# One attention turn in a new sequence on all five engines, with both row sends of a tile behind TensorE's query transposes

## The chip, the cores and the metric

The kernel runs on one core of one Trainium2 chip. The metric is the device time of one execution in microseconds (us); the span of a profiled execution is a little shorter than its time.

## The reference, cut to what matters

`x` is (64, 64, 256) and `ctx` is (64, 64, 256), both fp32. B = L = 64, D = 256, 16 heads of 16, 8 experts with inner size 176, two experts per token.

```python
q = rms_norm(linear(layernorm(x), q_w, q_b), norm_q_w)      # over all 256
k = rms_norm(linear(ctx, k_img_w, k_img_b), norm_k_img_w)
v = linear(ctx, v_img_w, v_img_b)
x = x + linear(attention(q, k, v), o_w, o_b)                # 16 heads, softmax(q k / 4) v
h = layernorm(x)
topw, sel = top_k(softmax(h @ gate_w.T), 2)                 # topw divided by its sum
out = x + sum over the two experts of topw * w2 @ (silu(g) * u)   # g, u = halves of w1 @ h
```

All context tokens fall under the image weights, since L is below 257; the text branch sees no tokens.

## The kernel before

**Stages.** 4096 tokens are 32 tiles of 128 tokens (two batches of 64). A first stage runs attention, the second LayerNorm and the routing, tile by tile, and writes each normalised row twice, once for each of its two experts, into `sorted_rows` in HBM, at a place that depends on the routing. A plan of 72 expert slots follows, then the expert stage reads `sorted_rows` slot by slot and writes `expert_out`; at the end both results of a token are added to `x1`. The change touches the first stage alone.

**Turns.** `turns_sp(eng, turn)` calls `turn(i // 4, i % 4)` for i = 0 to 37 (`LAST`) on every engine; all is unrolled. In turn i an engine works on several tiles at once: `tile(lag)` is tile i - lag, and is left out where it is below 0 or above 31. The order in which `turn` names its steps is the order of the engine's instruction stream; each engine works through it strictly in that order, and semaphores join the engines. So one pass through the five lists is one turn, and takes each of six or more tiles a step further.

**TensorE (PE) in turn i:** `tr_x(i)` (transposes of the normalised input, L1134), `tr_k(i-1)` (L1143), `score_max(i-2)` (rough scores for the row maximum, L1165), `weigh(i-3)` (probabilities times v, 32 small matmuls, L1177), `tr_q(i-1)` (the query transposes, L1150), `project_kv(i)`, `project_q(i)` (helper lines L1117 to L1125), `tr_max(i-2)` (L1206), in odd turns `count_rows`, `tr_att(i-3)` (L1212), `score(i-2)` (L1227 to L1231), `project_out(i-3)` (L1117 to L1125).

**ScalarE (ACT):** `xt_hi(i)`, `k_hi(i-1)` (L554), `ln1_norm(i+1)`, `ctx_hi(i+1)` (L569), `q_hi(i-1)` (four copies, L564), `neg_max_rows(i-2)` (L586), `k_square(i)` (L593), `q_square(i)` (L599), `att_hi(i-3)`, `v_copy(i)`, `weights_hi(i)` (L574), `k_scale(i)` (waits for POOL's `r_qk`, L628), `row_copy(i-4)` (L581), `softmax_exp(i-2)` (L621), in odd turns `gap_exp`.

**VectorE (DVE):** `xt_lo(i)` (L829), `k_lo(i-1)` (L835), `find_max(i-2)` (L846), LayerNorm statistics of tile i+2, the negated maximum, `invert_sums` and `normalise(i-3)`, `q_lo(i-1)` (L841), `ln2_norm(i-4)` (L905), `att_lo(i-3)`, in odd turns `route`, `gate_of_x(i)`, `q_scale(i)` (waits for `r_qk`, L883), `residual(i-3)` (L892 to L896 and the aggregate L899), in even turns `choose` (the two experts of two tiles, L914 to L927).

**GpSimd (POOL):** `ctx_lo(i+1)` (L401), `ln1(i+2)` (L413, L415, L422), `qk_rms(i)` (`ms_eps` L413 and `r_qk` L415; waits for both squares of tile i), in even turns `weights` of two tiles (L442 to L446), `send(i-6)`: a copy of the row numbers (L451) and two indirect DMAs of 128 rows (L457), `ln2(i-3)` (L413, L415), `weights_lo(i)` (L407).

**SyncE (SP)** issues `load_ctx(i+2)`, `load_weights(i+1)` and `spread_v(i)` (four DMAs, L335, which wait for `weighed` of tile i-2).

What binds these lists across engines: `weigh(i-3)` and `score_max(i-2)` wait for `softmax_exp(i-3)`, whose bank of scores `score_max` overwrites; `softmax_exp` stands behind `k_scale` in ACT's list; `tr_k` waits for `k_scale` of its tile; `tr_q` waits for `k_lo` of its tile. After the last turn the routing counts go through 15 small steps on DVE, and SP reads the first 12 rows of the plan into registers (L361) before it waits for all sends and loads the first slot.

Of the kernel before, what the change touches and what calls it, by code (L numbers as in the profile page):

```python
# [7 lines left out]
ALU = mybir.AluOpType  # L8
# [10 lines left out]
B, L, D = 64, 64, 256  # L19
# [66 lines left out]
def build_in(nc, stack, x, ctx_t, w_proj, w_out, w_exp, w_gate, bias, norm_q, norm_k, out,  # L86
# [216 lines left out]
    def _(sp):  # L303
# [39 lines left out]
        def turn(j, s):  # L343
            if Tile(j, s + 2).live:
                load_ctx(Tile(j, s + 2))
# [9 lines left out]

        turns_sp(sp, turn)
# [30 lines left out]
    def _(pool):  # L387
# [37 lines left out]
        def qk_rms(t):  # L425
# [3 lines left out]
            inv_sqrt(t, r_qk[:, t.par, :], ms_eps[:, t.par, :], sumsq[:, t.par, :], 1.0 / D, 1e-6,  # L429
                     S["k_squared"], S["qk_veps"], S["qk_rstd"])  # L430

        def ln2(t):
            need_alone(pool, pool_passed, S["row_ready"], t.n - 1)
            inv_sqrt(t, rstd2[:, t.slot, :], veps2[:, t.par, :], mean_var2[:, t.par, 1:2], 1.0, 1e-5,
                     S["ln2_mean"], S["ln2_veps"], S["ln2_rstd"])
# [12 lines left out]
        def send(t):  # L448
# [3 lines left out]
                             ).then_inc(S["ids_set"], 1)  # L452
            need_alone(pool, pool_passed, S["ids_set"], t.n + 1)
            need_alone(pool, pool_passed, R["place_set"], t.pair + 1)
            need_alone(pool, pool_passed, R["weight_set3"], t.pair + 1)
            for k in range(2):
                pool.indirect_dma_start(  # L457
                    sorted_rows, bass.IndirectOffsetOnAxis(ap=place_i[:, t.slot // 2, k, t.par:t.par + 1], axis=0),
                    row[:, k, t.slot, :], None, bounds_check=ROWS - 1, oob_is_err=False
                ).then_inc(row_sent[t.slot], 16)  # L460
# [985 lines left out]
```

## Time and profile before

| | |
|---|---|
| median of 3 runs | 549.66 us (548.14 to 552.85) |
| the profiled execution: its time, its span | 549.9 us, 548.1 us |
| granted TensorE clock, mean over the span | 0.938 of full |
| PE, PEld, DVE busy | 438.2, 389.1, 413.4 us |
| ACT, POOL busy | 315.5, 303.5 us |

How to read it: the times of the three runs and that of the profiled execution are of the whole program; busy time is the time in which an engine had an instruction running, and PEld (weight loads) overlaps PE. The first stage runs from the start to about 337 us, the expert stage from about 352 us.

### The profile page before, as it was taken

To read this page: it belongs to the slowest core of one execution; us is meant where nothing else is said; L and a number is where in the kernel's file an instruction comes from. 1 tells how busy PE (TensorE), PEld (TensorE's weight loads), DVE (VectorE), ACT (ScalarE), POOL (GpSimd) and SP (SyncE) were. 2 spreads that over 40 slices of the span, in tenths; PEclk is the share of its full clock that TensorE was granted. 3 is DMA by queue.
4 is the path that set the end of the run, shared out by engine and by line. 5 is a ranking of instruction groups with operands and counts; after the bars stand their busy time and mean duration, and the time that the engine had idled before them with its cause. 6 is when DMAs were issued, how large, how long until landed. Compare 5 with 4: busy or idle time off the path is not lost.

```text
span 548.1 us, 14646 instructions
## 1 busy us (share of the span) xinstructions
PE 438.2 (80%) x4120; PEld 389.1 (71%) x4120; DVE 413.4 (75%) x1359; ACT 315.5 (58%) x934; POOL 303.5 (55%) x531
## 2 busy tenths in 40 slices
PE   2879889898989998898989772299999999999100
PEld 1668778777877877787778661199999999899100
DVE  7458888988988898889888867066767676676384
ACT  5357777767776867686777531155656666565000
POOL 6634467777777677767776646224444444444200
PEclk9989999999999999999999986599999999999655
DMA  7231432222322222222222113524444444331499
GB/s 232 53 111 40 133 129 83 73 65 80 88 67 72 74 82 73 77 78 77 79 72 74 50 50 94 149 81 129 124 123 126 119 121 126 111 115 66 168 401 351
DMA packets 49560, 60.51 MB, mean 110 GB/s; under 512 B 7616, under 2 KB 43083, under 8 KB 49483
## 3 DMA queue, kind: packets, MB, share of 16 engines
q1 hardware_dynamic: 38026, 38.00, 23.7%
q0 software_dynamic: 6528, 16.86, 8.8%
q10 hardware_dynamic: 4928, 4.72, 2.6%
q8 instruction: 37, 0.61, 0.5%
q14 instruction: 41, 0.33, 0.2%
HBM read 32.86 MB, written 23.27 MB: 102 GB/s over the span
## 4 chain that ended last, share of the span: by engine, by line
PE 62%; DVE 12%; issue 7%; ACT 5%; POOL 5%; DMA 4%; SPq 2%; another core or an unknown queue 0%; POOLq 0%; ACTq 0%; DVEq 0%
PE bank L1117 11%; PE bank L1118 11%; PE bank L1119 11%; PE bank L1328 4%; DMA we_l<-expert_out 3%; PE bank L1177 3%; PE bank L1125 3%; PE bank L1150 3%; PE bank L1227 2%; DVE late L835 2%; PE bank L1231 2%; PE bank L1228 2%; PE bank L1229 2%; PE bank L1165 2%; PE bank L1357 1%
## 5 line engine op out<-in xcount | busy, mean ns | idle before, releaser
L527 POOL DMA_INDIRECT expert_out<-probs,late x72 | 70.0, 972 | 94.4 <-ACT probs L720 60.1
L457 POOL DMA_INDIRECT sorted_rows<-row,place_i x64 | 66.0, 1031 | 36.2 <-POOL row L451 24.5
L564 ACT CAST qp_h<-bank 32x256 f16<-32x256 f32 x128 | 46.4, 363 | 40.8 <-PE bank L1150 38.5
L841 DVE TENSOR_TENSOR qp_l<-bank,qp_h 32x256 f16<-32x256 f32 x128 | 53.7, 419 | 9.8 <-ACT qp_h L564 6.6
L1117 PE MATMUL bank<-we_h,xt_h 128*128 x144 | 53.4, 371 | 0.1
L1075 DVE SCALAR_TENSOR_TENSOR probs<-xn,late,bank 128x128 f32<-128x128 f32 x72 | 25.0, 347 | 36.2 <-issue 16.9
L708 ACT ACTIVATE xn<-bank 128x176 f32<-128x176 f32 x72 | 22.9, 318 | 42.7 <-PE bank L1119 35.2
L1118 PE MATMUL bank<-we_l,xt_h 128*128 x144 | 47.1, 327 | 0.0
L1119 PE MATMUL bank<-we_h,xt_l 128*128 x144 | 46.9, 326 | 0.0
L1067 DVE TENSOR_TENSOR xt_l<-bank,xt_h 128x256 fp32r<-128x256 f32 x72 | 30.5, 424 | 21.3 <-ACT xt_h L702 17.5
L1328 PE MATMUL bank<-ident,late 128*128 128x128 f32 x144 | 30.4, 294 | 18.4 <-DMA late<-sorted_rows 16.2
L415 POOL TENSOR_TENSOR rstd<-veps,half_neg 128x1 f32<-128x1 f32 x64 | 36.8, 575 | 5.5 <-POOL veps L413 0.2
L846 DVE TENSOR_REDUCE bank<-bank 128x16 f32<-128x1024 f32 x32 | 39.1, 1221 | 0.0
L702 ACT CAST xt_h<-bank 128x256 fp32r<-128x256 f32 x72 | 27.1, 376 | 18.9 <-PE bank L1328 18.4
L1227 PE MATMUL bank<-qp_h,late 128*128 128x256 f16 x128 | 35.7, 279 | 2.5 <-ACT neg_max_t L586 0.4
L720 ACT COPY probs<-bank 128x256 f32<-128x256 f32 x72 | 26.8, 373 | 17.6 <-PE bank L1358 10.5
L1177 PE MATMUL bank<-v_bd,probs 128*64 128x34 f32 x1024 | 36.0, 225 | 0.2 <-ACT probs L621 0.2
L1231 PE MATMUL bank<-neg_max_t,head_of 128*128 128x128 bf16 x256 | 35.6, 221 | 0.0
L1228 PE MATMUL bank<-qp_l,late 128*128 128x256 f16 x128 | 35.3, 276 | 0.0
L1229 PE MATMUL bank<-qp_h,late 128*128 128x256 f16 x128 | 35.3, 276 | 0.0
L1177 PEld LDWEIGHTS bank<-v_bd,probs 128*64 128x64 f32 x1024 | 32.4, 138 | 3.6 <-ACT probs L621 0.4
L621 ACT ACTIVATE probs<-bank 128x1024 f32<-128x1024 f32 x32 | 32.8, 1025 | 2.3 <-PE bank L1231 2.3
(199 smaller groups left out, 1594.7 us busy)
## 6 DMA issues: line engine op xcount, KB each, us to landing
late<-sorted_rows SPq DMA_DIRECT2D x72, 129.0 KB
we_f<-w_exp SPq DMA_DIRECT2D x32, 152.0 KB
v_bd<-v_sb SPq DMA_DIRECT2D x128, 34.0 KB, 1.9
ctx_in<-ctx_t SPq DMA_DIRECT2D x32, 128.0 KB
we_h<-expert_out SPq DMA_DIRECT2D x8, 512.0 KB, 6.8
we_l<-expert_out SPq DMA_DIRECT2D x8, 512.0 KB, 15.7
x<-x SPq DMA_DIRECT2D x3, 1024.0 KB, 5.8
out<-we_h ACTq DMA_DIRECT2D x8, 256.0 KB, 13.0
```

The costliest lines, as they stand in the source:

```text
L457: pool.indirect_dma_start(sorted_rows, bass.IndirectOffsetOnAxis(ap=place_i[:, t.slot // 2, k, t.par:t.par + 1], axis=0), row[:, k, t.slot ...
L527: pool.indirect_dma_start(expert_out, bass.IndirectOffsetOnAxis(ap=hs[:, r, D:D + 1].bitcast(U32), axis=0), y_sb[:, r % YRING, :], None, b ...
L564: act.copy(q_part(qp_h, t, g), q_bank(g)).then_inc(S["q_h_ready"], 1)
L841: dve.tensor_tensor(q_part(qp_l, t, g), q_bank(g), q_part(qp_h, t, g), ALU.subtract).then_inc(S["q_l_ready"], 1)
L1117: pe.matmul(dst, a_h, b_h, start=start, stop=False)
L1118: pe.matmul(dst, a_h, b_l, start=False, stop=False)
L1119: return pe.matmul(dst, a_l, b_h, start=False, stop=stop)
L1177: ins = pe.matmul(av_bank[b * L:(b + 1) * L, g * 2 * VW:(g + 1) * 2 * VW], probs[:, t.par, at:at + L], v_bd[:, t.par, b, :, g * VW:(g + 1) ...
L1227: pe.matmul(dst, k_h, q_h, start=True, stop=False)
L1228: pe.matmul(dst, k_h, q_l, start=False, stop=False)
L1231: ins = pe.matmul(dst[:, gh * P:(gh + 1) * P], head_of[:, (b * KC + c) * NQ // 2 + gh, :], neg_max_t[:, t.par, :], start=False, stop=gh == ...
L1328: ins = pe.transpose(bank[:, p, c * P:(c + 1) * P], hs[:, r, c * P:(c + 1) * P], ident[:, :])
```

## The change

The five lists are reordered. Nothing that is computed changes.

- **POOL:** `send` is split. `set_ids(i-5)` (the copy of the row numbers) ends the turn; the two indirect DMAs of tile i-6 now open the next turns' lists, behind a new wait of POOL for `q_transposed`, min(i, 32), which `tr_q(i-1)` raises in the same turn. Behind them stand `ln2_veps(i-4)`, `ctx_lo(i+2)`, `ln1_root(i+2)`, `ln2_root(i-4)`, and only then `qk_rms(i)`. `weights` moves to odd turns and to the end, `ln2` is a tile later.
- **ACT:** `weights_hi` moves up behind `q_hi`, `ctx_hi` is a tile further ahead and stands behind `neg_max_rows`, `ln1_norm` stands behind `att_hi`, `gap_exp` ahead of `k_scale`, `softmax_exp` ahead of `row_copy`, and `k_hi(i)`, `xt_hi(i+1)` end the turn.
- **DVE:** `k_lo` stands ahead of `xt_lo`; the aggregate of the second LayerNorm leaves `residual` and becomes `ln2_mean(i-4)`; the first LayerNorm's statistics are a tile further ahead; `ln2_norm` stands behind `route`, `q_scale` ahead of `gate_of_x`.
- **PE:** `weigh` stands ahead of `score_max`, `tr_max` between `project_kv` and `project_q`, and `tr_k(i)`, `tr_x(i+1)` end turn i (`tr_k` first).
- **SP:** `load_ctx` is a tile further ahead. A few steps of the first tiles move ahead of turn 0.

```diff
@@ SP
         def turn(j, s):
-            if Tile(j, s + 2).live:
-                load_ctx(Tile(j, s + 2))
+            if Tile(j, s + 3).live:
+                load_ctx(Tile(j, s + 3))
...
+        load_ctx(Tile(0, 2))
@@ POOL
-        def send(t):
+        def set_ids(t):
             need_alone(pool, pool_passed, S["row2_ready"], t.n + 1)
             pool.tensor_copy(row[:, :, t.slot, D:D + 1].bitcast(I32), result_row[:, :, bass.ds(t.n, 1)]
                              ).then_inc(S["ids_set"], 1)
+
+        def send(t, k):
             need_alone(pool, pool_passed, S["ids_set"], t.n + 1)
             need_alone(pool, pool_passed, R["place_set"], t.pair + 1)
             need_alone(pool, pool_passed, R["weight_set3"], t.pair + 1)
-            for k in range(2):
-                pool.indirect_dma_start(...)
+            pool.indirect_dma_start(...)
...
         def turn(j, s):
-            if Tile(j, s + 1).live:
-                ctx_lo(Tile(j, s + 1))
+            i = j * SKEW + s
+            if Tile(j, s - 6).live:
+                need(pool, S["q_transposed"], min(i, NT))
+                send(Tile(j, s - 6), 0)
+                send(Tile(j, s - 6), 1)
+            if Tile(j, s - 4).live:
+                ln2_veps(Tile(j, s - 4))
             if Tile(j, s + 2).live:
-                ln1(Tile(j, s + 2))
+                ctx_lo(Tile(j, s + 2))
+            if Tile(j, s + 2).live:
+                ln1_root(Tile(j, s + 2))
+            if Tile(j, s - 4).live:
+                ln2_root(Tile(j, s - 4))
             if Tile(j, s).live:
                 qk_rms(Tile(j, s))
-            if s % 2 == 0 and Tile(j, s - 6).live:
-                weights(Tile(j, s - 6), Tile(j, s - 5), (s - 6) // 2 % 2)
-            if Tile(j, s - 6).live:
-                send(Tile(j, s - 6))
-            if Tile(j, s - 3).live:
-                ln2(Tile(j, s - 3))
             if Tile(j, s).live:
                 weights_lo(Tile(j, s))
+            if Tile(j, s + 2).live:
+                ln1_shift(Tile(j, s + 2))
+            if s % 2 == 1 and Tile(j, s - 5).live:
+                weights(Tile(j, s - 5), Tile(j, s - 4), (s - 5) // 2 % 2)
+            if Tile(j, s - 5).live:
+                set_ids(Tile(j, s - 5))
@@ ACT
-            xt_hi(tile(0)); k_hi(tile(1)); ln1_norm(tile(-1)); ctx_hi(tile(-1))
             q_hi(tile(1))
+            weights_hi(tile(0))
             neg_max_rows(tile(2))
+            ctx_hi(tile(-2))
             k_square(tile(0)); q_square(tile(0)); att_hi(tile(3))
+            ln1_norm(tile(-1))
             v_copy(tile(0))
-            weights_hi(tile(0))
+            if s % 2 == 1: gap_exp(tile(5), tile(4), ...)
             k_scale(tile(0))
+            softmax_exp(tile(2))
             row_copy(tile(4))
-            softmax_exp(tile(2))
-            if s % 2 == 1: gap_exp(tile(5), tile(4), ...)
+            k_hi(tile(0)); xt_hi(tile(-1))
@@ DVE
-            xt_lo(tile(0)); k_lo(tile(1)); find_max(tile(2)); ln1_stats(tile(-2))
-            neg_max_hi(tile(2)); invert_sums(tile(3)); neg_max_lo(tile(2)); normalise(tile(3)); ln1_mean(tile(-2))
-            q_lo(tile(1)); ln2_norm(tile(4)); att_lo(tile(3)); route(...)
-            gate_of_x(tile(0)); q_scale(tile(0)); residual(tile(3)); choose(...)
+            k_lo(tile(1)); xt_lo(tile(0)); find_max(tile(2)); ln2_mean(tile(4))
+            neg_max_hi(tile(2)); neg_max_lo(tile(2)); invert_sums(tile(3)); ln1_mean(tile(-2)); ln1_stats(tile(-3)); normalise(tile(3))
+            q_lo(tile(1)); att_lo(tile(3)); route(...); ln2_norm(tile(4))
+            q_scale(tile(0)); gate_of_x(tile(0)); residual(tile(3)); choose(...)
@@ PE
-            tr_x(tile(0)); tr_k(tile(1)); score_max(tile(2)); weigh(tile(3)); tr_q(tile(1))
-            project_kv(tile(0)); project_q(tile(0)); tr_max(tile(2))
+            weigh(tile(3)); score_max(tile(2)); tr_q(tile(1))
+            project_kv(tile(0)); tr_max(tile(2)); project_q(tile(0))
             count_rows(...); tr_att(tile(3)); score(tile(2)); project_out(tile(3))
+            tr_k(tile(0)); tr_x(tile(-1))
```

The parts for ACT, DVE and PE are written here one call behind the other, without their `if tile(n).live`.

## Rows read from the trace of the kernel before

**Rows 1.** The page: busy time of each engine.

```profile
PE 438.2 (80%) x4120; PEld 389.1 (71%) x4120; DVE 413.4 (75%) x1359; ACT 315.5 (58%) x934; POOL 303.5 (55%) x531
```

**Rows 2.** Stretches A:B (us): length, busy per engine, granted clock, DMA share.

```profile
191.81:210.57 18.76, 17.11 (x195) 14.68 (x191) 16.65 (x60) 13.50 (x40) 13.99 (x28) 1.00 0.27 75
310.00:320.00 10.00, 7.52 (x97) 6.12 (x96) 7.58 (x23) 5.90 (x14) 6.97 (x12) 1.00 0.17 55
```

**Rows 3.** Timeline of PE: query transposes of tiles 5, 21, 22, 23, 31.

```profile
71.09 0.41 PE L1150 MATMUL bank<-ident,late 128*128 128x128 f32 x2 [0.17 <-DVE late L835]
...
220.33 0.41 PE L1150 MATMUL bank<-ident,late 128*128 128x128 f32 x2 [0.17 <-issue]
...
230.01 0.41 PE L1150 MATMUL bank<-ident,late 128*128 128x128 f32 x2 [0.91 <-DVE late L835]
...
238.94 0.41 PE L1150 MATMUL bank<-ident,late 128*128 128x128 f32 x2 [0.17 <-issue]
...
313.45 0.44 PE L1150 MATMUL bank<-ident,late 128*128 128x128 f32 x2
```

**Rows 4.** Timeline of PE: what stands ahead of the transposes at 230.01.

```profile
227.44 0.61 PE L1165 MATMUL bank<-late,qp_h 128*128 128x128 f16 x8 [0.29 <-ACT probs L621]
227.98 1.13 PE L1177 MATMUL bank<-v_bd,probs 128*64 128x34 f32 x32
```

**Rows 5.** Timeline of ACT: k_scale, row copy, exponential, k_hi, two q_hi.

```profile
225.60 0.47 ACT L628 ACTIVATE late<-bank,r_qk 128x256 f32<-128x256 f32 x1 [0.38 <-POOL r_qk L415]
225.97 0.40 ACT L581 COPY row<-row 128x256 f32<-128x256 f32 x1
226.27 1.02 ACT L621 ACTIVATE probs<-bank 128x1024 f32<-128x1024 f32 x1
...
227.44 0.61 ACT L554 CAST late<-bank 128x512 f16<-128x512 f32 x1
...
230.79 1.52 ACT L564 CAST qp_h<-bank 32x256 f16<-32x256 f32 x4 [1.96 <-PE bank L1150]
...
239.38 1.52 ACT L564 CAST qp_h<-bank 32x256 f16<-32x256 f32 x4 [0.52 <-PE bank L1150]
```

**Rows 6.** Timeline of POOL in one turn, and one second send.

```profile
217.59 1.09 POOL L457 DMA_INDIRECT sorted_rows<-row,place_i  x1 [0.82 <-POOL row L451]
218.98 0.97 POOL L457 DMA_INDIRECT sorted_rows<-row,place_i  x1 [0.30 <-DVE mean_var L899]
220.02 0.19 POOL L413 TENSOR_SCALAR veps<-mean_var 128x1 f32<-128x1 f32 x1
220.29 0.57 POOL L415 TENSOR_TENSOR rstd<-veps,half_neg 128x1 f32<-128x1 f32 x1
...
221.65 0.74 POOL L401 TENSOR_TENSOR ct_l<-ctx_in,ct_h 128x256 fp32r<-128x256 f32 x1
...
224.58 0.19 POOL L413 TENSOR_SCALAR ms_eps<-sumsq 128x2 f32<-128x2 f32 x1 [0.80 <-ACT square L599]
224.86 0.71 POOL L415 TENSOR_TENSOR r_qk<-ms_eps,half_neg 128x2 f32<-128x2 f32 x1
...
229.13 0.97 POOL L457 DMA_INDIRECT sorted_rows<-row,place_i  x1 [0.30 <-issue]
```

**Rows 7.** Timeline in the expert stage: the copy on ACT that POOL's indirect DMA awaits.

```profile
402.50 0.37 ACT L720 COPY probs<-bank 128x256 f32<-128x256 f32 x1 [0.23 <-PE bank L1358]
...
403.64 0.97 POOL L527 DMA_INDIRECT expert_out<-probs,late  x1 [1.06 <-issue]
```

**Rows 8.** Timeline of DVE at the end of that turn: residual, and k_lo.

```profile
226.53 0.42 DVE L892 TENSOR_TENSOR x<-bank,x 128x256 f32<-128x256 f32 x1 [0.45 <-PE bank L1125]
...
229.19 0.68 DVE L835 TENSOR_TENSOR late<-bank,late 128x512 f16<-128x512 f32 x1
```

**Rows 9.** The chain that ended last: SP's register loads, then the first slot's load.

```profile
349.58 0.15 SPq L361
...
350.13 2.15 DMA late<-sorted_rows
```

More of the change, by code:

```diff
@@ L495, in _ @@
                                  base=0, pattern=[[1, NE], [-1, NE]], channel_multiplier=0))
-        ln1(Tile(0, 0))
-        ln1(Tile(0, 1))
+        for n in range(2):
+            ln1_root(Tile(0, n))
+            ln1_shift(Tile(0, n))
         ctx_lo(Tile(0, 0))
@@ L521, in _ @@
                         ).then_inc(q_cleared, 1)
+        ctx_lo(Tile(0, 1))
         turns_sp(pool, turn)
@@ L645, in tile @@
                 return t
-            if tile(0).live:
-                xt_hi(tile(0))
-            if tile(1).live:
-                k_hi(tile(1))
-            if tile(-1).live:
-                ln1_norm(tile(-1))
-            if tile(-1).live:
-                ctx_hi(tile(-1))
             if tile(1).live:
@@ L693, in _ @@
         ln1_norm(t)
+        xt_hi(t)
+        ctx_hi(Tile(0, 1))
         split_hi(1)
@@ L989, in turn @@
                 route(tile(5), tile(4), (s - 5) // 2 % 2)
-            if isinstance(j, int) and j == s == 0:
+            if tile(4).live:
+                ln2_norm(tile(4))
+            if n == 0:
                 fold_gate()
             if tile(0).live:
+                q_scale(tile(0))
+            if tile(0).live:
                 gate_of_x(tile(0))
-                q_scale(tile(0))
             if tile(3).live:
@@ L1284, in seen @@
                 return min(value, NT) if static else value
-            if tile(0).live:
-                tr_x(tile(0))
-            if tile(1).live:
-                tr_k(tile(1))
+            if tile(3).live:
+                weigh(tile(3))
             if tile(2).live:
@@ L1293, in turn @@
                 score_max(t)
-            if tile(3).live:
-                weigh(tile(3))
             if tile(1).live:
                 tr_q(tile(1))
-            if tile(0).live:
+            if static and i == 0:
                 t = tile(0)
-                t.first = static and i == 0
-                for project_next in (project_q, project_kv) if t.first else (project_kv, project_q):
-                    project_next(t)
-            if static and i == 0:
+                t.first = True
+                project_q(t)
+                project_kv(t)
                 gate_fold()
+            elif tile(0).live:
+                t = tile(0)
+                t.first = False
+                project_kv(t)
             if tile(2).live:
@@ L1308, in turn @@
                 tr_max(t)
+            if tile(0).live and not (static and i == 0):
+                t = tile(0)
+                t.first = False
+                project_q(t)
             if s % 2 == 1 and tile(5).live:
@@ L1318, in turn @@
                 project_out(t)
+            if tile(0).live:
+                tr_k(tile(0))
+            if tile(-1).live:
+                tr_x(tile(-1))
         gate_mean()
+        tr_x(Tile(0, 0))
         turns_sp(pe, turn)
```

74 lines of the change are left out of this document (42 added, 32 removed).

## The prediction

> **What bounds the kernel now.** I read the page first: PE is busy 80% and DVE 75% of the span, POOL 55% [rows 1]. None is full, so the windows come next. Over two whole turns of 18.76 us PE is busy 17.11 and DVE 16.65 us, ACT and POOL some 14 us, at granted clock 1.00 [rows 2]: a turn costs 9.4 us, of which PE works 8.6 and DVE 8.3. From the query transposes of tile 5 to those of tile 31 there are 26 turns and 313.45 - 71.09 = 242.4 us [rows 3], 9.32 us a turn. The turns alternate: 230.01 - 220.33 = 9.68 us where DVE's `choose` stands ahead of `k_lo`, and 238.94 - 230.01 = 8.93 us where it doesn't [rows 3]. PE loses two things in a turn: 0.29 us waiting for the exponential ahead of `score_max` [rows 4], and 0.17 or 0.91 us waiting for `k_lo` ahead of `tr_q` [rows 3]. The reader is to see how small this is: if both went, 0.46 and 1.20 us, a turn would cost 8.5 us on PE, and no order can give back more than (9.32 - 8.5) x 26 = 21 us.
>
> POOL is not on this loop now. Its `qk_rms` sits idle 0.80 us until the query square is there [rows 6], then `k_scale` starts 0.03 us after `r_qk` [rows 5, 6]. The sends stand behind `qk_rms`, where nothing of the same turn waits for what follows them.
>
> **The change, what it removes.** `k_lo` ahead of `xt_lo` and the aggregate taken out of `residual` bring `k_lo` forward by some 0.4 us. `softmax_exp` ahead of `row_copy` brings the exponential forward by 0.30 us (226.27 - 225.97) [rows 5]. Both aim at PE's two waits; alone they would give most of 0.8 us in a long turn and 0.3 in a short one. `tr_max` ahead of `project_q`, `weights_hi` and `ctx_hi` in ACT's idle time cost and give nothing by themselves: ACT has 1.96 or 0.52 us of idle ahead of `q_hi` [rows 5] and the new steps fill it. `weigh` ahead of `score_max` moves work among neighbours; `find_max` gets its scores a `weigh` later, but it has the negated maximum due only after `project_kv`. `load_ctx` has more than a turn of slack.
>
> **What it adds: a loop through POOL.** This is the term that decides. In turn i POOL now waits for `tr_q(i-1)` of the same turn, sends twice, does four steps, and only then computes `r_qk(i)`; ACT's `k_scale(i)` and, behind it in the list, `softmax_exp(i-2)` wait for that; `weigh(i-2)` and `score_max` on PE wait for the exponential; behind them stands `tr_q(i)`, for which POOL waits again. All steps are in one order on their engine, so the sum of this loop is a floor for the turn. With 0 at the end of `tr_q(i-1)`:
> - From the wait to the first indirect DMA: 0.77 us, the distance from the end of the copy that POOL awaits to its DMA in the expert stage (403.64 - 402.87) [rows 7]; in this stage 0.82 us stand behind the copy of row numbers [rows 6]. I take 0.80.
> - The two sends: 1.09 + 0.30 + 0.97 = 2.36 us, and 0.07 to the next step (220.02 - 219.95) [rows 6]. At 3.23.
> - `ln2_veps` 0.19, `ctx_lo` 0.74, `ln1_root` 0.27 + 0.57, `ln2_root` 0.57, `qk_rms` 0.28 + 0.71 [rows 6]: 3.33 us, less some 0.06 of overlaps. `r_qk` is there at 6.5 us. Before it was there at 225.57 - 220.74 = 4.83 us [rows 3, 6].
> - `k_scale` starts at 6.53, the exponential one step of 0.37 us (225.97 - 225.60) later, at 6.90, and takes 1.02 [rows 5]: 7.92 us.
> - PE begins `weigh` 0.15 us after it (227.44 - 227.29) [rows 4, 5], at 8.07. `weigh` and `score_max` take 229.11 - 227.44 = 1.67 us together [rows 4] and `tr_q` 0.41, less 0.06 of overlap: 10.09 us.
>
> In even turns `choose` makes it longer. `q_scale` starts with `k_scale` at 6.53, `residual` about 0.6 later at 7.12. From `residual` to `k_lo` it is 2.66 us now (229.19 - 226.53) [rows 8]; without `xt_lo` (0.34 of issue) and without the aggregate (about 0.2) it is 2.1. `k_lo` ends at 7.12 + 2.1 + 0.68 = 9.9, PE starts `tr_q` 0.14 later and ends it at 10.45. In odd turns `k_lo` is not late: ACT does the row copy and `k_hi` (0.61) [rows 5] behind the exponential and is done at 8.7, `k_lo` at 9.4, while PE is busy until 9.7. Mean of both turns: 10.27 us, against 9.32.
>
> What hid the sends before was that they stood behind `qk_rms`; that cover is gone, and the 0.80 us of wake-up comes on top because a wait now stands right ahead of them. ACT and DVE idle in the new turn: the exponential starts at 226.27 - 220.74 = 5.53 us now [rows 3, 5], so the scores of tile i-2 are there by then, and it waits behind `k_scale` until 6.9. What is queued behind POOL's wait is its whole list; `weights_lo` takes 0.8 us (221.65 - 220.86) [rows 6], `weights` and `set_ids` together 1.4: from `r_qk`'s end at 225.57 to the second send at 229.13 it is 3.56 us, less the lead, the first send and the gap [rows 6]. `weights` also needs the row copy, which ends near 8.2. All of it ends near 9.6, before the next wait, and adds nothing.
>
> **How many turns.** The first send is in turn 6, and its loop sets the `tr_q` of turn 7; the last loop is that of turn 31. That is 26 turns, the same that I measured: 26 x (10.27 - 9.32) = +24.7 us. In turns 1 to 5 nothing is sent and the two shorter waits count: between 0 and 2 us back, I take 1. At the end earlier sends win little: SP loads its registers until 349.73 us and starts the first slot's load at 350.13 [rows 9], so the sends can't have held it for more than 0.4 us. The sum: 549.9 (the profiled execution, 0.2 above the median) + 24.7 - 1 = 573.6; I say 573.
>
> **Rivals.**
> (1) The wake-up is hidden: POOL prepares the first indirect DMA while the wait is pending, and only the descriptor work comes behind `tr_q`. Then a turn is 9.47 us, 26 x 0.15 = +4, less 1: 553 us. Against it: POOL was idle for 1.06 us ahead of the DMA in the expert stage and still began it 0.77 us after the copy's end [rows 7]; nothing had been prepared. The trace doesn't agree in its 0.77 us, so by that rule this rival keeps only a small chance.
>
> (2) Faster: the loop through POOL doesn't bind, because a send does not hold up what stands behind it. Then the turn falls to what DVE needs, 8.33 busy and about 0.55 of small gaps, 8.9 us: 26 x 0.42 = 11 us less, with the 1 us of the start 538 us. It decides if POOL's next instruction can start within 0.5 us of the first send. Against it: the next one starts 0.07 us after the second send's end (220.02 - 219.95) [rows 6].
>
> (3) Worse, by contention: PE's signals come late while sends run. In the turn where the second send ended at 230.10, `q_hi` started 0.78 us after the start of `tr_q`; where it ended well before, 0.44 us after [rows 3, 5, 6]. If PE's signals between 0.9 and 3.9 us were all held until 0.7 us after the second send, `neg_max_rows` and `ctx_hi` would start near 3.9 and `ctx_lo` 1.0 us late: 11.3 us a turn, 599 us. In part, or with the clock falling because PE idles 1.5 us a turn, 585 to 600. Against it: PE is busy 75% between 310 and 320 us at granted clock 1.00 [rows 2], and will be busy 8.5 of 10.3 us, 83%.
>
> **How the numbers follow.** Forecast 0.73, with its own range 563 to 582 (a turn of 9.9 to 10.6 us, the start 0 to 2 us); rival 1 0.08; rival 2 0.09; rival 3 0.10. A measurement of this kernel can tell about 1% from no change. Below 544.2 lies rival 2 and little else: faster 0.09. Within 1%, 544.2 to 555.2, lies rival 1: same 0.08. Slower: 0.83. The range must leave out no more than 2 in 10: 555 to 586 holds the forecast, a part of rival 3 and the edge of rival 1.
>
> **What would show it.** Right: a turn of 10 to 10.5 us between query transposes from tile 6 on; POOL's first send 0.8 us behind the end of `tr_q`; `ms_eps` no longer idle for the square but directly behind `ln2_root`; ACT idle ahead of `k_scale` for more than 1.5 us, its releaser `r_qk`; PE idle ahead of `tr_k` and of `weigh`. Turns 1 to 5 below 9 us. Wrong: `r_qk` there before 5.5 us, a send that starts within 0.3 us of `tr_q`'s end, or sends shorter than 0.9 us. It would also be wrong if the long turns, through `choose`, turned out as short as the others, by 4 us.

## The result, and the profile after

The changed kernel takes 585.5 us (median of 4 runs, 583.7 to 588.0), the kernel before 549.1 us beside it: a ratio of 1.066, 95% interval 1.062 to 1.070. The profiled execution took 583.7 us with a span of 581.9 us, that of before 549.9 and 548.1 us. So 33.8 us have to be found, where 23.7 were forecast.

Busy time first (the page), to be held against [rows 1]:

```profile
PE 452.9 (78%) x4120; PEld 397.7 (68%) x4120; DVE 409.1 (70%) x1359; ACT 323.9 (56%) x934; POOL 301.6 (52%) x531
```

The instruction counts are the same and POOL and DVE have no more work. PE is busy 14.7 us longer with the same 4120 matmuls, and the other 19 of the 33.8 us are idle time of PE. Its clock is about half of the 14.7: where the granted clock is 1.00, two turns show 17.4 to 17.5 us of PE busy against 16.9 to 17.0 before, some 7 us over 26 turns, and the rest is in stretches of lower clock. The windows (us of the stretch, busy time of PE, PEld, DVE, ACT and POOL, granted clock, DMA share, GB/s) say where:

```profile
73.42:328.30 254.88, 216.67 (x2271) 183.09 (x2269) 196.33 (x696) 168.62 (x480) 165.38 (x326) 0.96 0.24 71
...
233.03:254.70 21.67, 19.40 (x193) 16.16 (x192) 16.47 (x59) 14.06 (x40) 13.76 (x27) 0.89 0.23 66
```

Timeline of PE, the query transposes of tiles 5, 19, 20, 29, 31, to be held against [rows 3]:

```profile
73.42 0.41 PE L1178 MATMUL bank<-ident,late 128*128 128x128 f32 x2
...
221.46 0.41 PE L1178 MATMUL bank<-ident,late 128*128 128x128 f32 x2
...
233.03 0.63 PE L1178 MATMUL bank<-ident,late 128*128 128x128 f32 x2
...
328.30 0.41 PE L1178 MATMUL bank<-ident,late 128*128 128x128 f32 x2
...
346.20 0.41 PE L1178 MATMUL bank<-ident,late 128*128 128x128 f32 x2
```

From tile 5 to tile 31 it is 346.20 - 73.42 = 272.8 us against 242.4: +30.4. Tile 5 comes at 73.42 instead of 71.09: +2.3. From tile 31's transposes to the end of the span it is 235.7 against 234.65: +1.05. That is the 33.8 us. The turns are 10.24 us (odd) and 10.72 (even, with `choose`) where nothing else happens. Some are longer (233.03 - 221.46 = 11.57), and the last two take 346.20 - 328.30 = 17.9 together.

One turn on POOL, counted from the end of `tr_q` at 221.87, to be held against [rows 6]:

```profile
222.70 1.09 POOL L467 DMA_INDIRECT sorted_rows<-row,place_i  x1 [1.00 <-PE bank L1178]
224.10 0.98 POOL L467 DMA_INDIRECT sorted_rows<-row,place_i  x1 [0.31 <-issue]
...
225.41 0.73 POOL L402 TENSOR_TENSOR ct_l<-ctx_in,ct_h 128x256 fp32r<-128x256 f32 x1
...
226.51 1.11 POOL L419 TENSOR_TENSOR rstd<-veps,half_neg 128x1 f32<-128x1 f32 x2
227.71 0.19 POOL L414 TENSOR_SCALAR ms_eps<-sumsq 128x2 f32<-128x2 f32 x1
227.98 0.70 POOL L419 TENSOR_TENSOR r_qk<-ms_eps,half_neg 128x2 f32<-128x2 f32 x1
```

The first send begins 0.83 us behind `tr_q`, nothing but work stands between it and `r_qk`, and `r_qk` ends at 6.81 us. The same turn on ACT and PE, against [rows 4, 5]:

```profile
224.09 0.41 ACT L590 CAST ct_h<-ctx_in 128x256 fp32r<-128x256 f32 x1
...
228.71 0.47 ACT L649 ACTIVATE late<-bank,r_qk 128x256 f32<-128x256 f32 x1 [2.02 <-POOL r_qk L419]
229.09 1.02 ACT L642 ACTIVATE probs<-bank 128x1024 f32<-128x1024 f32 x1
```

```profile
229.24 0.73 PE L1171 MATMUL bank<-ident,late 128*128 128x128 f32 x4 [1.65 <-ACT late L649]
...
230.34 1.93 PE L1205 MATMUL bank<-v_bd,probs 128*64 128x34 f32 x32
```

ACT stands 2.02 us for `r_qk`, then PE 1.65 us for `k_scale`. And `weigh` behind it takes 1.93 us instead of 1.13 [rows 4]: between 230.30 and 233.66 the granted clock is 0.50, the lower of PE's two levels (1.2 and not 2.4 GHz). The page's groups (busy us, mean ns, idle just before them and who ended it) give the whole run's bill:

```profile
L467 POOL DMA_INDIRECT sorted_rows<-row,place_i x64 | 66.0, 1031 | 78.5 <-PE bank L1178 64.4
L1171 PE MATMUL bank<-ident,late 128*128 128x128 f32 x128 | 21.5, 292 | 41.9 <-ACT late L649 41.8
L649 ACT ACTIVATE late<-bank,r_qk 128x256 f32<-128x256 f32 x32 | 15.2, 474 | 37.5 <-POOL r_qk L419 37.5
L402 POOL TENSOR_TENSOR ct_l<-ctx_in,ct_h 128x256 fp32r<-128x256 f32 x32 | 23.5, 733 | 23.2 <-ACT ct_h L590 21.4
```

The first three are the predicted loop. In the kernel before, the wait of `k_scale` for `r_qk` was 14.0 us in all and that of `tr_k` for `k_scale` 2.3:

```profile
L628 ACT ACTIVATE late<-bank,r_qk 128x256 f32<-128x256 f32 x32 | 15.2, 474 | 14.0 <-POOL r_qk L415 14.0
```

The fourth isn't in the prediction. An early turn, before any send, shows it (`r_qk` in the row below it ends 60.44 - 54.52 = 5.92 us behind `tr_q`, 4.83 before):

```profile
57.22 0.74 POOL L402 TENSOR_TENSOR ct_l<-ctx_in,ct_h 128x256 fp32r<-128x256 f32 x1 [1.31 <-ACT ct_h L590]
...
59.74 0.70 POOL L419 TENSOR_TENSOR r_qk<-ms_eps,half_neg 128x2 f32<-128x2 f32 x1
```

`ctx_lo(i+2)`, ahead of `qk_rms` on POOL, waits for `ctx_hi(i+2)` of the same turn on ACT, and that stands behind `q_hi(i-1)`, hence behind `tr_q(i-1)`. It is a second loop, with no send in it. Of its 21.4 us, 21.1 lie in the first turns, before any send; behind the sends `ct_h` is there in time (224.50 against `ct_l` at 225.41 above), and this loop sets nothing.

### The profile page after: what moved, and what is told of

Same layout as the page of the kernel before. It is cut to its first block and busy times, and to the rows that moved or that the text cites. A ratio compares the mean times of both kernels' runs of the same rounds, so it can differ in the third digit from the quotient of the medians.

```text
span 581.9 us, 14710 instructions
## 1 busy us (share of the span) xinstructions
PE 452.9 (78%) x4120; PEld 397.7 (68%) x4120; DVE 409.1 (70%) x1359; ACT 323.9 (56%) x934; POOL 301.6 (52%) x531
## 5 line engine op out<-in xcount | busy, mean ns | idle before, releaser
L1171 PE MATMUL bank<-ident,late 128*128 128x128 f32 x128 | 21.5, 292 | 41.9 <-ACT late L649 41.8
L1171 PEld LDWEIGHTS bank<-ident,late 128*128 128x128 f32 x128 | 13.7, 143 | 48.3 <-ACT late L649 48.3
L1364 PE MATMUL bank<-ident,late 128*128 128x128 f32 x144 | 30.8, 297 | 18.3 <-DMA late<-sorted_rows 16.5
L1205 PEld LDWEIGHTS bank<-v_bd,probs 128*64 128x64 f32 x1024 | 34.0, 143 | 9.1 <-ACT probs L642 9.0
L1205 PE MATMUL bank<-v_bd,probs 128*64 128x34 f32 x1024 | 37.7, 230 | 1.6 <-ACT probs L642 0.5
L744 ACT COPY probs<-bank 128x256 f32<-128x256 f32 x72 | 26.8, 372 | 17.4 <-PE bank L1394 11.9
L649 ACT ACTIVATE late<-bank,r_qk 128x256 f32<-128x256 f32 x32 | 15.2, 474 | 37.5 <-POOL r_qk L419 37.5
L402 POOL TENSOR_TENSOR ct_l<-ctx_in,ct_h 128x256 fp32r<-128x256 f32 x32 | 23.5, 733 | 23.2 <-ACT ct_h L590 21.4
```

Of the source, the lines that this page charges most:

```text
L1205: ins = pe.matmul(av_bank[b * L:(b + 1) * L, g * 2 * VW:(g + 1) * 2 * VW], probs[:, t.par, at:at + L], v_bd[:, t.par, b, :, g * VW:(g + 1) ...
L1364: ins = pe.transpose(bank[:, p, c * P:(c + 1) * P], hs[:, r, c * P:(c + 1) * P], ident[:, :])
```

## The experiments

Theory A is the prediction's: what stands on GpSimd between `tr_q` and `r_qk` is added up. Its rivals are named in each expectation. The kernel before took 547.5 to 550.6 us beside these runs.

**v1_no_wait: the wait alone is taken out.**

```diff
             if Tile(j, s - 6).live:
-                need(pool, S["q_transposed"], min(i, NT))
                 send(Tile(j, s - 6), 0)
```

> The changed kernel with one line out: POOL no longer waits for q_transposed ahead of the two sends. Theory A (the loop tr_q, wait, two sends, four steps, r_qk, k_scale, exponential, weigh, tr_q sets the turn): the loop is cut, POOL sends as soon as set_ids and the weights are done. What is left is a second, shorter loop, seen in turns 1 to 5 where nothing is sent: tr_q, q_hi, ct_h on ACT, ctx_lo, the roots, r_qk 5.9 us behind tr_q; a turn of 9.4 to 9.8 us and a time of 552 to 562 us. Theory B (sends beside the projections cost by contention, the wait itself nothing): 575 to 586, since the sends still lie near the same place. Theory C (the new order of the other engines costs): 575 to 586.

Measured: 582.0 us, ratio 1.060 (1.056 to 1.063). Theory A missed by 20 us: the kernel gains 3.5 us and not 25. The number lies in the range that B and C share, and can't tell them apart. Timeline of POOL over two turns, and one row each of PE and ACT:

```profile
209.65 1.11 POOL L467 DMA_INDIRECT sorted_rows<-row,place_i  x1 [0.81 <-POOL row L459]
211.07 0.97 POOL L467 DMA_INDIRECT sorted_rows<-row,place_i  x1 [0.30 <-issue]
...
215.37 0.72 POOL L402 TENSOR_TENSOR ct_l<-ctx_in,ct_h 128x256 fp32r<-128x256 f32 x1 [1.05 <-ACT ct_h L589]
...
217.91 0.73 POOL L419 TENSOR_TENSOR r_qk<-ms_eps,half_neg 128x2 f32<-128x2 f32 x1
...
220.51 0.19 POOL L450 TENSOR_SCALAR one_e<-e_gap 128x2 f32<-128x2 f32 x1 [0.83 <-ACT row L601]
...
222.72 1.09 POOL L467 DMA_INDIRECT sorted_rows<-row,place_i  x1 [0.81 <-POOL row L459]
```

```profile
211.19 0.41 PE L1177 MATMUL bank<-ident,late 128*128 128x128 f32 x2 [0.36 <-DVE late L858]
```

```profile
212.70 1.53 ACT L584 CAST qp_h<-bank 32x256 f16<-32x256 f32 x4 [2.55 <-PE bank L1177]
```

Each kind of turn fails for its own reason. In the one that the first rows show, the sends do run before `tr_q` ends at 211.60, but `q_hi` starts only at 212.70, 0.66 us behind the second send's end, and hands 1.1 us to `ctx_hi`, `ctx_lo` and `r_qk`, which ends 7.04 us behind `tr_q`. In the next, `weights` waits for the row copy, so the copy of the row numbers ends at 221.91, the send begins 0.81 us later, and that is 0.6 us behind `tr_q` anyway. What it now waits for is the row numbers instead of `tr_q`. So a part of theory B is true: signals beside the sends come late in every second turn.

**v2_sends_behind_qk and v3_wait_alone.** Both have the sends where they stood before, behind `qk_rms`; the second keeps the wait at the head of the turn.

```diff
             if Tile(j, s - 6).live:
-                need(pool, S["q_transposed"], min(i, NT))      # kept in v3
-                send(Tile(j, s - 6), 0)
-                send(Tile(j, s - 6), 1)
 ...
                 qk_rms(Tile(j, s))
+            if Tile(j, s - 6).live:
+                send(Tile(j, s - 6), 0)
+                send(Tile(j, s - 6), 1)
```

> The changed kernel, with POOL's two sends behind qk_rms and without the wait. Theory A: as without the wait, 552 to 562 us, r_qk 5.9 us behind tr_q; a little less if POOL's list has slack. Theory B: below 549. Theory C: 575 to 586.

> The changed kernel, with the wait for q_transposed left at the head of POOL's turn but the two sends behind qk_rms. It tells the wait from what stands between it and r_qk. Theory A: within 3 us of the same kernel without the wait (552 to 562), because POOL then waits for ct_h anyway, which comes 2.7 us behind tr_q. A rival A2 (any wait of POOL for tr_q is what costs): 575 to 586.

Measured: 577.4 us, 1.051 (1.048 to 1.055), and 576.6 us, 1.050 (1.046 to 1.054). The wait by itself costs nothing here: the two agree within 1 us, as A said of v3, and A2 falls, since v2 has no wait. But A's 552 to 562 us is missed by 15 us in both, and the place of the sends gives back only 8 of the 36 us. 577 us is what theory C (the other engines' new order costs) had forecast; it is v6 below, with the same order of the other engines at 549.5 us, that rules C out. POOL and DVE of v2 in the long turn:

```profile
221.56 0.73 POOL L402 TENSOR_TENSOR ct_l<-ctx_in,ct_h 128x256 fp32r<-128x256 f32 x1 [0.91 <-ACT ct_h L589]
...
226.36 0.97 POOL L467 DMA_INDIRECT sorted_rows<-row,place_i  x1 [0.31 <-issue]
227.35 0.84 POOL L408 TENSOR_TENSOR we_l<-we_f,we_h 128x304 fp32r<-128x304 f32 x1
```

```profile
226.76 1.46 DVE L943 TENSOR_TENSOR gap<-top 128x2 f32<-128x2 f32 x1
```

Two things have taken the sends' place. The second loop is seen in the first row: `ct_l` waits 0.91 us for `ct_h`, `r_qk` ends 5.9 to 6.0 us behind `tr_q`, and the odd turns take 9.47 us. And in the even turns, 11.12 us long, the sends now run beside `choose`, whose subtraction of two columns takes 1.46 us; L918 took 0.14 us in the kernel before (mean 142 ns of 16). `k_lo` and `tr_q` stand behind it.

**v4_sends_alone: the sends' new place in the kernel before.** All other engines keep the old order.

```diff
         def turn(j, s):
+            if Tile(j, s - 6).live:
+                need(pool, S["q_transposed"], min(i, NT))
+                send(Tile(j, s - 6))              # both indirect DMAs
             if Tile(j, s + 1).live:
                 ctx_lo(Tile(j, s + 1))
 ...
+            if s % 2 == 1 and Tile(j, s - 5).live:
+                weights(Tile(j, s - 5), Tile(j, s - 4), (s - 5) // 2 % 2)
+            if Tile(j, s - 5).live:
+                set_ids(Tile(j, s - 5))
```

> The kernel before with one part of the change alone: the two sends open POOL's turn behind the wait for q_transposed, weights and the copy of row numbers end the turn before; all other engines as before. Theory A: r_qk 6.2 us behind tr_q instead of 4.8, and ACT still has the row copy ahead of the exponential: a turn of 10.1 to 10.6 us, 568 to 582 us. Theory C (it is the other engines' order that costs): 545 to 553.

Measured: 610.0 us, 1.109 (1.105 to 1.113), far beyond the expectation. The windows of its 26 turns and of one long turn, and the wait in that turn:

```profile
70.73:374.34 303.61, 254.19 (x2455) 216.73 (x2456) 226.62 (x750) 174.16 (x515) 178.09 (x345) 0.87 0.22 63
...
259.02:271.57 12.55, 9.79 (x93) 8.36 (x93) 9.26 (x33) 6.58 (x19) 7.36 (x15) 0.88 0.18 57
```

```profile
266.93 0.66 PE L1150 MATMUL bank<-ident,late 128*128 128x128 f32 x4 [1.97 <-ACT late L635]
```

The turn costs 11.7 us against 9.3. The sends alone, in the old order of the other engines, do more harm than the whole change: its other reorderings are not what is slow. The clock makes it worse. PE idles 1.97 us in this turn ahead of `tr_k`, and 0.66 more ahead of `score_max`; the granted clock of the stretch is 0.87, and PE's busy time in it 254 us against 219 for the same matmuls before.

**v5_exp_first: ACT's exponential ahead of `k_scale`.**

```diff
                 v_copy(tile(0))
+            if tile(2).live:
+                softmax_exp(tile(2))
 ...
                 k_scale(tile(0))
-            if tile(2).live:
-                softmax_exp(tile(2))
```

> The changed kernel with ACT's exp of the scores (and the gap's exp) ahead of k_scale instead of behind it. In the changed kernel's turn GpSimd's r_qk ends 6.81 us after tr_q, k_scale takes 0.3, and the exp runs from 7.22 to 8.24; ACT idles 2.02 for r_qk. Theory A (the loop runs through GpSimd's r_qk, k_scale, tr_k and weigh): the exp no longer stands behind r_qk, weigh's other condition stays PE's own order behind tr_k, which waits for k_scale; so only about 0.3 of a turn goes or nothing, 26 turns: 575 to 585 us against 585.5. Theory B (the exp's late end is what holds weigh): the turn loses some 1 us, 555 to 563 us.

Measured: 582.5 us, 1.058 (1.053 to 1.063), as theory A. Moving the exponential alone gives 3 us. `tr_k` and `tr_x`, which PE has to do ahead of `weigh`, wait for `k_scale` as well. In an odd turn of the changed kernel `tr_x` ends 8.18 us behind `tr_q` and the exponential 8.17: there are two ways from `r_qk` to `weigh`, equally long, and taking one away leaves the other.

**v6_short_path: the same sends, the same wait, `r_qk` earlier.** This is the decisive run.

```diff
                 ln2_veps(Tile(j, s - 4))
+            if Tile(j, s - 4).live:
+                ln2_root(Tile(j, s - 4))
+            if Tile(j, s).live:
+                qk_rms(Tile(j, s))
             if Tile(j, s + 2).live:
                 ctx_lo(Tile(j, s + 2))
             if Tile(j, s + 2).live:
                 ln1_root(Tile(j, s + 2))
-            if Tile(j, s - 4).live:
-                ln2_root(Tile(j, s - 4))
-            if Tile(j, s).live:
-                qk_rms(Tile(j, s))
```

> The changed kernel with GpSimd's steps in another order alone: both sends stay at the head, behind the wait for tr_q, but r_qk is taken right behind ln2's root, ahead of the low part of the context and of ln1's root. Theory A (a sum along the loop: everything on GpSimd between the sends and r_qk is on it): r_qk ends 1.7 us earlier, at about 5.1 us behind tr_q, turns of 8.8 to 9.2, 547 to 558 us. Theory B (the sends themselves slow the engines beside them, TensorE's signals come late and its clock falls, wherever r_qk stands): the turn stays above 10 us, 572 to 585 us.

Measured: 549.5 us, 0.998 (0.996 to 1.001), as theory A: all of the 36 us are gone. Timeline of POOL behind the `tr_q` that ends at 209.59:

```profile
210.41 1.09 POOL L467 DMA_INDIRECT sorted_rows<-row,place_i  x1 [2.21 <-PE bank L1180]
211.81 0.97 POOL L467 DMA_INDIRECT sorted_rows<-row,place_i  x1 [0.30 <-issue]
...
213.77 0.19 POOL L414 TENSOR_SCALAR ms_eps<-sumsq 128x2 f32<-128x2 f32 x1
214.04 0.70 POOL L419 TENSOR_TENSOR r_qk<-ms_eps,half_neg 128x2 f32<-128x2 f32 x1
```

The sends begin 0.82 us behind `tr_q` as in the changed kernel, and `r_qk` ends at 5.15, where the changed kernel's odd turns have 6.75. In the even turns the row numbers are late, the sends begin at 1.41 and `r_qk` ends at 5.76 instead of 6.80. The turns are 8.73 (odd) and 9.92 us (even) instead of 10.24 and 10.72: 1.51 and 0.80 us less for 1.60 and 1.04 us less up to `r_qk`. The granted clock of the 26 turns is back at 1.00, and tile 5's transposes come at 68.56 us, 4.9 us earlier than in the changed kernel, since `ctx_lo` no longer stands ahead of `r_qk` in the first turns either.

**v7_ctx_early, v8_sends_apart, v9_lo_ahead: no loop through `r_qk`, and what the sends do to their neighbours.** All take `ctx_lo(i+1)` at the head of the turn and the sends behind `qk_rms`; they differ in what stands around the sends.

```diff
# v7:  ctx_lo(i+1), ln2_veps, ln1_root, ln2_root, qk_rms, send 0, send 1, weights_lo, ln1_shift, ...
# v8:  ctx_lo(i+1), ln2_veps, ln1_root, ln2_root, qk_rms, send 0, weights_lo, ln1_shift, send 1, ...
# v9:  ctx_lo(i+1), ln2_veps, ln1_root, ln2_root, qk_rms, weights_lo, ln1_shift, send 0, send 1, ...
```

> The changed kernel with the sends taken back behind qk_rms, without the wait, and the low part of the context taken one turn later, at the head of the turn, so that it doesn't wait for ACT's high part of the same turn. Theory A (two loops: the sends ahead of r_qk, worth 1.4 to 1.8 a turn; and context high part, low part, roots, r_qk, worth some 0.5): both are gone, odd turns of 9.0 to 9.2 and even ones of 9.2 to 10 (with what stays of the two-column subtraction that took 1.46 us beside the second send), 540 to 555 us. Theory B (the other engines' new order itself is slower): as with the sends behind qk_rms, 572 to 580 us.

> As the kernel with the context's low part a turn later and both sends behind qk_rms, but the second send stands behind weights_lo and ln1's shift: the sends aren't back to back. Theory A (only what stands ahead of r_qk counts): the same time within 1%. Theory C (two sends in a row hold VectorE's small two-input operations and TensorE's signals longer than two sends apart): faster by 0.3 to 1 us a turn, 8 to 25 us.

> As the kernel with the context's low part a turn later and both sends behind qk_rms (568.5 us, turns of 9.9 and 10.6 us), but weights_lo and ln1's shift stand ahead of the sends. There the two-column subtraction of the gap took 1.20 us in the mean, beside a send and weights_lo, against 0.14 in the kernel before. Theory A (weights_lo, a subtraction of two SBUF tiles on GpSimd, holds the gap's two-input subtraction on VectorE): weights_lo is over by then, the gap goes back to 0.14 to 0.25 us, the long turn loses 1 us or more, 548 to 558 us. Theory B (the sends hold it): it stays above 1 us and the time at 563 to 572 us.

Measured: 568.5 us, 1.030 (1.026 to 1.034); 559.6 us, 1.018 (1.011 to 1.026); 545.0 us, 0.990 (0.986 to 0.994). v7 lies between its two theories: A is missed by 13 us, though `r_qk` ends 4.7 to 4.8 us behind `tr_q` in one kind of turn and 5.6 to 6.0 in the other. v8 is 8.9 us faster than v7, at the low edge of its theory C. v9 is 3 us below the range of its theory A. DVE's groups show the reason, in v7, then v8, then v9:

```profile
L943 DVE TENSOR_TENSOR gap<-top 128x2 f32<-128x2 f32 x16 | 19.2, 1201 | 0.0
```

```profile
L948 DVE TENSOR_TENSOR chosen<-expert_no,top_no 128x16 f32<-128x16 f32 x32 | 11.1, 385 | 0.5
L952 DVE TENSOR_TENSOR chosen_b<-chosen 128x16 bf16<-128x16 f32 x16 | 8.0, 498 | 0.5
```

```profile
L964 DVE TENSOR_TENSOR place_of<-chosen,place 128x32 f32<-128x32 f32 x16 | 7.1, 442 | 0.0
...
L942 DVE TENSOR_TENSOR gap<-top 128x2 f32<-128x2 f32 x16 | 2.3, 143 | 0.0
```

It isn't one instruction that is slow but whichever small two-input one lies at the wrong time: `gap` in v7 (before: 142 ns), `chosen` and `chosen_b` in v8 (before: 172 and 207), `place_of` in v9 (before: 184). In v7 this makes `choose` hold back `k_lo`, and PE stands 2.0 us in the mean, 2.5 at most, ahead of `tr_q` in the 16 long turns (31.6 us in all); the clock falls too (mean over the run 0.902). In v9 the held instruction stands in `route`, where nothing waits for it, and the time falls below that of the kernel before. Which neighbour holds them? In v9 one turn has POOL's `weights_lo` and DVE's `place_of` side by side, with no send near:

```profile
155.84 0.84 POOL L408 TENSOR_TENSOR we_l<-we_f,we_h 128x304 fp32r<-128x304 f32 x1
```

```profile
155.96 0.76 DVE L964 TENSOR_TENSOR place_of<-chosen,place 128x32 f32<-128x32 f32 x1
```

`place_of` ends 0.04 us behind `weights_lo`; in another turn (174.52) it came 0.07 us ahead of `weights_lo` and took 0.18. The Trainium skill, SBUF — State Buffer, section "Who interferes with whom", says that a VectorE instruction with two SBUF inputs and a GpSimd instruction that reads SBUF exclude one another for the whole instruction; the trace agrees in this pair of rows. Theory B of v9 isn't disproved by that run, as `gap` fell between the two sends in it. The rows of v2 speak for B's part too: `gap` started 0.40 us into the second send and 0.59 us ahead of `weights_lo`, and still ended with `weights_lo`. So in its later part a send with `weights_lo` next on GpSimd holds such an instruction, and `weights_lo` keeps holding it. A send does not do it in every place, though. In the kernel before, where the second send follows, `gap` began 0.41 us into the first and took its 0.14:

```profile
227.74 1.09 POOL L457 DMA_INDIRECT sorted_rows<-row,place_i  x1 [0.81 <-POOL row L451]
```

```profile
228.15 0.14 DVE L918 TENSOR_TENSOR gap<-top 128x2 f32<-128x2 f32 x1
```

**v10_choose_late: v6, with `choose` in the next turn.**

```diff
                 xt_lo(tile(0))
+            if s % 2 == 1 and tile(5).live:
+                a = tile(5)
+                a.first = isinstance(j, int) and a.n == 0
+                choose(a, tile(4), (s - 5) // 2 % 2)
 ...
-            if s % 2 == 0 and tile(4).live:
-                a = tile(4)
-                a.first = isinstance(j, int) and a.n == 0
-                choose(a, tile(3), (s - 4) // 2 % 2)
```

> As the kernel with the short path to r_qk (549.5 us, turns of 8.73 and 9.92 us), but VectorE chooses the experts of a pair behind k_lo and xt_lo of the next turn instead of at the end of its own. In the long turn k_lo now waits for choose (1.5 us), and tr_q for k_lo by 0.59. Theory A: k_lo follows ACT's k_hi, tr_q the last score_max: the long turn loses 0.6, the following one gains nothing, 541 to 545 us. Theory B: find_max and tr_max come 1.4 us later in the following turn, and TensorE stands ahead of the query projection for it: 549 to 560 us.

Measured: 546.2 us, 0.991 (0.989 to 0.994), 3.4 us less than v6 where A gave 4.5 to 8.5. The turns of 8.73 and 9.92 have become 9.71 and 8.69: the long turn lost 1.23, but the next one gained 0.98. The time lies between the two theories, and each is right in part.

**v11_short_no_wait: v6 without the wait.**

```diff
             if Tile(j, s - 6).live:
-                need(pool, S["q_transposed"], min(i, NT))
-            if Tile(j, s - 6).live:
                 send(Tile(j, s - 6), 0)
```

> As the kernel with the short path to r_qk (549.5 us), without the wait for tr_q ahead of the sends. Theory A (the sum along GpSimd alone): the sends start when GpSimd is free, some 1.5 us earlier, r_qk then waits for ACT's squares at 3.3 us behind tr_q and ends at about 4.2 instead of 5.15; turns of 8.7 to 9.6: 540 to 548 us. Theory B (sends beside weigh, score_max and tr_q make TensorE's signals late, as without the wait in the changed kernel, where q_hi began 1.10 us behind tr_q's end): what r_qk gains is given back, turns of 9.3 to 10: 549 to 566 us.

Measured: 541.5 us, 0.986 (0.981 to 0.991), as theory A; this is the fastest of all, 1.4% below the kernel before. POOL, and ACT behind the `tr_q` that ends at 206.19:

```profile
205.62 1.09 POOL L467 DMA_INDIRECT sorted_rows<-row,place_i  x1 [0.82 <-POOL row L459]
...
209.80 0.19 POOL L414 TENSOR_SCALAR ms_eps<-sumsq 128x2 f32<-128x2 f32 x1 [0.90 <-ACT square L620]
210.08 0.70 POOL L419 TENSOR_TENSOR r_qk<-ms_eps,half_neg 128x2 f32<-128x2 f32 x1
```

```profile
206.23 1.52 ACT L585 CAST qp_h<-bank 32x256 f16<-32x256 f32 x4 [1.73 <-PE bank L1178]
```

The short turn falls from 8.73 to 8.26: the sends start 1.39 us earlier, `r_qk` ends at 4.59 instead of 5.15, and waits for ACT's square again, as in the kernel before [rows 6]. The signal of `tr_q` isn't late here although a send is running. The long turn is 9.77: its sends start 1.3 us behind `tr_q`, 0.81 us behind the row numbers, so there the wait for `tr_q` had hardly mattered (1.41 in v6).

**v12_all: v11 with v10's `choose`, the query projection ahead of `tr_max` in odd turns, and `set_ids` ahead of `weights`.**

```diff
+            if s % 2 == 1 and tile(0).live:
+                t = tile(0)
+                t.first = False
+                project_q(t)
             if tile(2).live:
                 t = tile(2)
                 t.first = static and i == 2
                 tr_max(t)
 ...
```

The cut shows the query projection alone.

> The kernel with the short path to r_qk and no wait (541.5 us, turns of 8.26 and 9.77), with the choice of experts taken behind k_lo and xt_lo of the next turn, TensorE's query projection ahead of tr_max in that turn, and set_ids ahead of the pair's weights on GpSimd. Theory A (in the long turn k_lo waits 0.7 us for choose, and tr_q 0.59 for k_lo; in the next one the projection fills the time in which tr_max waits for find_max): a pair of turns takes 17.4 instead of 18.0 us, 532 to 536 us. Theory B (the delay of find_max is handed on through neg_max to the exp, or through the squares to r_qk): nothing is gained, 540 to 548 us.

Measured: 544.2 us, 0.994 (0.992 to 0.996), as theory B. PE in the turn that holds `choose`:

```profile
209.48 0.23 PE L1234 MATMUL bank<-ident_b,neg_max 128*128 128x128 bf16 x1 [0.17 <-DVE neg_max L881]
210.32 0.44 PE L1240 MATMUL bank<-ident,att 128*128 128x128 f32 x2 [0.47 <-DVE att L894]
```

The turns are 9.47 and 8.70 against 9.77 and 8.26. The 1.3 us of `choose` have only moved: `find_max` starts 0.95 us behind `tr_q` instead of 0.31 ahead of it, and the negated maximum, the squares on ACT behind it and the attention's division all come later.

## Why the prediction came out as it did

The direction, the mechanism and its place were right. The size was short by a third: the forecast of 573 us lies 12.5 us below the median of 585.5, outside the 563 to 582 that the forecast gave itself. The whole range of 555 to 586, whose upper end was there for rival 3, holds the median with 0.5 us to spare; that is luck in part, as one of the errors below (2.6 us) goes the other way. Step by step, in the profiled executions:

- **From the wait to the first send, 0.80:** 0.83 us. **The sends, 2.36:** 2.38. **Nothing else on POOL waits:** right, `ms_eps` begins 0.09 us behind the roots.
- **`r_qk` at 6.5 us:** 6.75 to 6.81. The step mis-sized is the sum of the POOL steps, "3.33 us, less some 0.06 of overlaps": they took 3.54. The instructions had their durations, but 0.08 to 0.09 us lies between one and the next, also where the next doesn't need the result (`veps` to `ct_l`). The sum had two of these five gaps; only the two roots overlap, by 0.03.
- **From `r_qk` through the exponential to `weigh`:** the times are right, the path is half of it. The sum has PE waiting for the exponential alone and leaves out `tr_k` and `tr_x`, which now stand ahead of `weigh` and wait for `k_scale`. They were done at 8.18 us behind `tr_q` in an odd turn, the exponential at 8.17. That the sum came out is a coincidence of two equal paths; v5, which takes the exponential off, is only 3 us faster.
- **The end of `tr_q` at 10.09 in odd turns, 10.45 in even ones:** 10.24 and 10.72. Over 24 turns the mean of the two is 0.21 us too low: 5.0 us.
- **The clock.** I held rival 3's "with the clock falling" against PE's busy share and gave it 0.10. The 24 turns from 73.42 to 328.30 took 254.9 us; at 10.48 each they would have taken 251.5. Most of these 3.4 us are from turns like the one that ends at 233.03, in which `weigh` and `tr_q` ran at the lower level behind a wait of 1.65 us; 5 of the 24 transposes did. (The first of the five is also longer by its send, 1.25 us, which began 0.98 us behind `tr_q`.) That part of rival 3 was real. PE's busy share over a long stretch was no argument against it.
- **26 equal turns:** the last two take 17.9 us together and not 20.5, since `ctx_lo` and `ln1_root` of tile i+2 no longer exist in them and `r_qk` comes 1.3 us earlier. I had the loop's last turn right and its contents wrong: 2.6 us too many.
- **Turns 1 to 5 give back 1 us:** wrong in sign. Tile 5's transposes come 2.3 us later. The failed step is "`ctx_hi` in ACT's idle time cost and give nothing": I priced the move on ACT and didn't follow its consumer, `ctx_lo`, to its new place ahead of `r_qk`. v6 shows it: with `ctx_lo` behind `qk_rms` tile 5's transposes come at 68.56.
- **The tail, 0:** +1.05 us, not looked into further.

Together: 5.0 + 3.4 - 2.6 + 3.3 (from -1 to +2.3) + 1.05 = 10.15 us, which is the 10.1 us between 33.8 and 23.7.

**The rivals.** (1) The wake-up is not hidden: 0.81 to 0.83 us behind `tr_q` in every turn but the first with a send (0.98), 0.81 behind the row numbers where the wait is gone. (2) A send does hold up what stands behind it. (3) PE's late signals exist, but not where I put them. In the changed kernel `ct_h` starts 2.22 us behind `tr_q` and not 3.9; the late signals of v1 came from sends ahead of `tr_q`.

**Was the loop the cause?** v6 settles it: with the same sends, the same wait and the same other engines, 1.6 and 1.0 us less between `tr_q` and `r_qk` took 36 us off the median and 34.6 off the profiled span: the 26 turns from tile 5 to tile 31 went from 272.8 to 242.4 us, tile 5 came 4.9 us earlier, and the rest came 0.65 later. It doesn't prove that the prediction's price was the whole of it, as v2 and v3 show: with the sends away from the head, the loop over `ct_h` and the held `gap` keep 28 of the 36 us. Those are not costs of the changed kernel, whose `gap` takes 0.14 us; they are what comes next when its first limit is removed. What v4 showed beyond the upper end of its expectation, 28 us, is partly the clock (35 us more busy time of PE in its 26 turns, of which some overlaps idle time) and partly the sends of every second turn, which start 1.85 us behind `tr_q`; the split wasn't measured.

## What to carry to other kernels

When several engines run fixed lists turn by turn, follow every moved step to its consumer and write down, for the new order, every path that starts and ends at the same step; a step that is moved into another engine's idle time can still bring its consumer onto such a path. Where two paths join, write both down, even if one alone gives the right sum. An experiment that takes one limit away shows the next one, so a small gain (v2: 8 of 36 us) doesn't refute the theory; shortening the suspected path with everything else left in place (v6) does the telling. Where PE will have a long wait in every turn, give a lower clock in some turns a price and a chance of its own, whatever its busy share.

## What the runs showed of the hardware that was not expected

- **Small VectorE instructions with two SBUF inputs are held beside GpSimd, and whether a send holds them goes with what stands behind it.** 128x32 took 0.76 us instead of 0.18 in v9 with `weights_lo` alone beside it; in v6 `gap` took 0.44, with no send near, and ended with `weights_lo`. In v2, v3 and v7, where `weights_lo` follows the second send, every `gap` that began 0.39 us or more into that send was held until `weights_lo` was over (0.89 to 1.72 us instead of 0.14); the two that began at 0.12 were not. Where another send follows (the kernel before, v1, v11, v12), none of some 80 such instructions that began 0.4 us or more into the first send was held. With small steps behind the send both were seen: in v8 the pair of `chosen` that began at 0.31 us was held in most turns, in v9 `chosen_b` was free at 0.41 to 0.43 us and held at 0.44, and late in the stage `chosen` was free at 0.58 (v8). Why is open.
- **A signal of TensorE can come late beside an indirect DMA.** `q_hi` started 0.66 us behind the second send's end, 1.10 us behind the end of `tr_q` (v1); in the kernel before 0.69 us behind the second send's end [rows 5, 6]. In v11, with the first send running when `tr_q` ended, it started 0.04 us behind it. Two sends in a row aren't needed: in v8, where the second stands apart, `q_hi` started 0.52 us behind it and 0.25 behind `tr_q`. Why a send with the other one next doesn't do it is open.
- **The wake-up of an indirect DMA was about the same behind each releaser:** 0.81 to 0.83 us behind a PE signal, 0.81 to 0.88 behind a GpSimd copy (v1, v6), 0.77 behind an ACT copy [rows 7], against 0.17 where nothing is awaited (v8) and 0.30 from the first send to the second. Taking the wait for `tr_q` away did not shorten it; it only moved behind the row numbers.
- **The clock fell in single turns with PE busy 90% of them** (19.40 of 21.67 us at 0.89). The wait ahead of `tr_k` was 1.65 us in that turn, but waits of 1.64 to 1.69 in others left `tr_q` at full speed, so the wait alone doesn't tell which turn it is. In the turn before 233.03 the granted clock was 1.00 up to the end of the wait (221.87 to 229.24) and 0.50 from 230.30 to 233.66. With v6's waits, 0.84 us at most ahead of `tr_k`, it stayed at 1.00 over all 26 turns.
